# Two units of attention per round of TensorE: scores of both, projections, values of both

## The reference

```
# layer 1 (causal)                              # layer 3 (biased)
q, k, v = x @ W_Q, x @ W_K, x @ W_V             q, k, v = h @ Wq, h @ Wk, h @ Wv
s = where(causal, q k^T, -1e10) / sqrt(64)      s = q k^T / sqrt(16) + rel_bias[buckets]
x = layernorm(x + softmax(s) v W_O)             x = layernorm(x + softmax(s) v Wo)
```

## Time and profile before

| | us |
|---|---|
| median of 3 runs | 4693.07 (4691.93 to 4693.48) |
| the profiled execution | 4695.17 |
| its span, first to last instruction | 4693.4 |

### The profile page before, as it was taken

How to read it: one execution, slowest core, us unless ns; L and a number is a source line. 1 busy time by engine, 2 the same in 40 slices (tenths; PEclk the granted TensorE clock), 3 DMA queues, 4 the chain that set the end, 5 groups by cost and what they waited for, 6 DMA issues and landing times. The chain is left out here.

```text
span 4693.4 us, 63371 instructions
## 1 busy us (share of the span) xinstructions
PE 4113.2 (88%) x22554; PEld 2146.0 (46%) x22554; DVE 3458.5 (74%) x5816; ACT 1969.6 (42%) x3446; POOL 2788.1 (59%) x2036
## 2 busy tenths in 40 slices
PE   5999999999868999989999848999999999999964
PEld 3554454544445555555555424444444444444423
DVE  3877887878667777777877637887888788878836
ACT  2443443434445445445454313444344344434422
POOL 0655655556625677776786915665666566656640
PEclk6999999999978999999999958999999999999987
DMA  2000000000020000000000021211112111112111
GB/s 51 13 14 13 23 13 22 14 9 5 1 71 18 26 26 26 27 26 26 31 26 9 5 58 24 39 30 28 36 28 41 28 37 28 31 25 45 18 46 36
DMA packets 98041, 125.90 MB, mean 27 GB/s; under 512 B 28896, under 2 KB 76448, under 8 KB 97728
## 3 DMA queue, kind: packets, MB, share of 16 engines
q1 hardware_dynamic: 97728, 121.86, 11.8%
HBM read 103.69 MB, written 18.12 MB: 26 GB/s over the span
## 5 line engine op out<-in xcount | busy, mean ns | idle before, releaser
L729 POOL TENSOR_TENSOR s_psum_p<-s_psum_p,s_prob 128x1024 f32<-128x1024 f32 (+3 forms) x640 | 1350.2, 2110 | 415.5 <-ACT s_prob L476 376.7
L476 ACT ACTIVATE s_prob<-s_sT 128x1024 f32<-128x1024 f32 (+2 forms) x896 | 835.9, 933 | 970.4 <-DVE s_sT L610 479.8
L384 PE MATMUL s_pv<-s_prob,s_vp 128*64 128x512 f32 (+3 forms) x3584 | 889.0, 575 | 3.9 <-POOL s_prob L714 3.0
L729 POOL TENSOR_TENSOR s_psum_p<-s_prob 128x1024 f32<-128x1024 f32 (+1 forms) x128 | 286.9, 2241 | 573.5 <-ACT s_prob L476 570.8
L615 DVE RECIPROCAL s_recip<-s_recip 128x128 f32<-128x128 f32 x512 | 480.8, 941 | 99.3 <-ACT s_recip L426 99.3
L340 PE MATMUL s_mx<-s_bh,s_ah 64*128 64x512 f32 (+3 forms) x1792 | 390.7, 431 | 183.0 <-DVE s_bm L551 84.6
L1613 POOL TENSOR_TENSOR s_psum_p<-s_psum_p,s_prob 128x1024 f32<-128x1024 f32 x192 | 464.3, 2418 | 111.4 <-ACT s_prob L1340 109.5
L561 DVE CUSTOM_DVE_ANT_0 s_mx<-s_mx,s_strip 128x512 f32<-128x512 f32 x640 | 429.1, 711 | 111.9 <-PE s_mx L340 110.9
L1340 ACT ACTIVATE s_prob<-s_sT 128x1024 f32<-128x1024 f32 x256 | 262.6, 1026 | 478.0 <-PE s_sT L1200 474.1
L1455 DVE SCALAR_TENSOR_TENSOR s_part<-s_sT,s_gate,s_part 128x128 f32<-128x128 f32 x945 | 287.4, 322 | 213.1 <-ACT s_part L1332 180.6
L359 PE MATMUL s_sT<-s_ah,s_bh 64*128 64x512 f32 (+3 forms) x1792 | 414.4, 459 | 19.1 <-ACT s_prob L476 18.8
(11 more groups left out here) (251 smaller groups left out, 7560.4 us busy)
## 6 DMA issues: line engine op xcount, KB each, us to landing
s_strip<-bias_rows SPq DMA_DIRECT2D x256, 144.0 KB, 5.7
s_wr<-gated_weights SPq DMA_DIRECT2D x32, 960.0 KB, 4.8
s_near<-bias_rows SPq DMA_DIRECT2D x256, 48.0 KB, 2.0
x<-s_x SPq DMA_DIRECT2D x12, 512.0 KB, 3.2
s_x<-x SPq DMA_DIRECT2D x8, 512.0 KB, 4.7
gated_weights<-s_side_hi SPq DMA_DIRECT2D x8, 480.0 KB, 2.5
gated_weights<-s_side_lo SPq DMA_DIRECT2D x8, 480.0 KB, 2.9
s_x<-in_L_attn_x_dram SPq DMA_DIRECT2D x4, 512.0 KB, 4.3
```

The source lines that it names most:

```text
L384: last = mm(pv[heads(hd), lo:CH], vp[:, g % 2, j, heads(hd)], prob[:, k % PR, hd, lo:CH], start=j == 0, stop=end)
L476: nc.scalar.activation(prob[:, k % PR, :, lo:CH], sT[:, k % 2, :, lo:CH], ACT.Exp, scale=st.scale).then_inc(exp_done, 1)
L729: nc.gpsimd.tensor_tensor(out[:, :, lo:CH], src, p[:, :, lo:CH], ALU.add)\
```

## The change

The causal and the biased stage now walk their units two at a time ("a block"): units u and u+1 with u even. The gated stage keeps its own program.

- TensorE's order in a block: a chunk of maxima, scores of k, scores of k+1, a chunk of maxima, side jobs of the first unit, values of k-2 and of k-1, side jobs of the second unit.
- Every unit has exactly one chunk. A lead of 2 (causal) or 4 (biased) chunks of group g+2 is done in the last units of group g; the stage's prologue does them for group 1.
- "mt" becomes a side job and uses `misc` instead of `mx`; it stands at unit 10 (causal) or 12 (biased).
- The copy of the bias columns moves from VectorE to ScalarE (`bias_columns`, job "dc" at unit 8, semaphore `dc_done`), so `m_per` is 2.
- VectorE's order in a block: chunk of the first unit, near biases of both units, low part left from the block before, chunk of the second unit (and `head_maxima` after the last), side jobs of the first unit, then reciprocals, normalization and layer norm of both units.
- ScalarE's: both exponentials, side jobs of the first unit, copy of finished values, side jobs of the second unit, then "dc" and "cut".
- New places for the jobs. In an ordinary group: item 0, 4, 6, 8, v 2, 10, rs 3, 11 (biased); item 0, 2, 4, 6, v 5, 8, rs 3, 7 (causal). Reciprocals of a group's first pass at 13, 14, 14, 15 (biased) or 8 to 11 (causal), of its second pass in the next group at 5, 6, 6, 7. The first pass is normalized at unit 1 of the next group, the second at unit 7.

```diff
+        self.lead = 2 if causal else 4
+        self.mt_unit = 14
...
         if g + 1 < GP:
-            for u, count in enumerate(self.mx_steps):
-                out[u] += [("mx", g + 1, n + k) for k in range(count)]
-                n += count
-            out[self.mt_unit].append(("mt", g + 1))
+            for u in range(self.U - self.lead):
+                out[u].append(("mx", g + 1, u + self.lead))
+            out[self.U - self.lead].append(("mt", g + 1))
+            if self.biased:
+                out[8].append(("dc", g + 1))
+        if g + 2 < GP:
+            for n in range(self.lead):
+                out[self.U - self.lead + n].append(("mx", g + 2, n))
...
+        plan = {"item": (0, 4, 6, 8), "v": (2, 10), "rs": (3, 11)}
+        if turn:
+            plan = {"v": (1, 2), "xt": (3, 4), "rs": (5, 11), "item": (6, 7, 8, 9)}
+        elif after:
+            plan = {"item": (0, 2, 4, 6), "rs": (3, 11), "v": (5, 7), "y": (8, 10), "t": (14, 15)}
+        if self.causal:
+            plan = {"item": (0, 2, 4, 6), "rs": (3, 7), "v": (5, 8)}
+            if turn:
+                plan = {"v": (1, 2), "xt": (3, 4), "rs": (5, 7), "item": (6, 7, 8, 9)}
+            elif after:
+                plan = {"item": (0, 2, 4, 6), "rs": (3, 7), "v": (1, 5), "y": (8, 9), "t": (10, 11)}
...
-        for s, u in ((2 * g - 1, 3), (2 * g, rs1 + 1)):
-            if s >= 0:
-                for n in range(4):
-                    out[u + n].append(("recip", s, n))
-                out[u + 4 if u + 4 < self.U else u + 3].append(("norm", s))
+        if g > 0:
+            for n, u in enumerate((5, 6, 6, 7)):
+                out[max(u, plan["rs"][0] + 1)].append(("recip", 2 * g - 1, n))
+            out[7].append(("norm", 2 * g - 1))
+        for n, u in enumerate((8, 9, 10, 11) if self.causal else (13, 14, 14, 15)):
+            out[u].append(("recip", 2 * g, n))
+        if g > 0:
+            out[1].append(("norm", 2 * g - 2))
         if p == 1 and b > 0:
-            for n in range(7):
-                out[(3 if self.causal else 5) + n].append(("ln", b - 1, n))
+            for n, u in enumerate((3, 4, 5, 6, 7, 8, 10) if self.causal else (5, 6, 7, 8, 9, 10, 12)):
+                out[u].append(("ln", b - 1, n))
...
 # TensorE
-            for g, u, k, c, j, todo in units():
-                scores(g, u, k, c, j)
-                chunks = [t for t in todo if t[0] == "mx"]
-                for t in chunks[:1]:
+            for g, u, k, first, second in blocks():
+                for t in of_kind(first, ("mx",)):
                     maxima(t[1], t[2])
-                if k >= 2:
-                    values(k - 2)
-                for t in todo:
-                    if t[0] in MISC:
-                        misc_job(t)
-                for t in chunks[1:]:
+                for n in range(2):
+                    scores(k + n)
+                for t in of_kind(second, ("mx",)):
                     maxima(t[1], t[2])
-                if ("mt", g + 1) in todo:
-                    m_transpose(g + 1)
+                for t in of_kind(first, MISC):
+                    misc_job(t)
+                if k > 0:
+                    for n in range(2):
+                        values(k - 2 + n)
+                for t in of_kind(second, MISC):
+                    misc_job(t)
...
 # ScalarE
+            def bias_columns(g):
+                if g == 0:
+                    act.wait_ge(set_up, 2)
+                elif g >= 2:
+                    act.wait_ge(mt_full, g - 1)
+                hs = slice(2 * (g % NPAIR), 2 * (g % NPAIR) + 2)
+                copy(m8[:, g % 2, :, NB:3 * NB], dcol[:, hs, :, :].rearrange("p a b n -> p a (b n)"))\
+                    .then_inc(dc_done, 1)
...
+                for n in range(2):
+                    exponentials(k + n)
+                for t in of_kind(first, MISC):
+                    misc_job(t)
                 if tail_pass(k) is not None:
                     copy_values(tail_pass(k))
...
 # VectorE
-            for g, u, k, c, j, todo in units():
-                for t in todo:
+            for g, u, k, first, second in blocks():
+                for t in of_kind(first, ("mx",)):
+                    maxima(t[1], t[2])
+                for n in range(2):
+                    if st.near(*st.units[u + n]):
+                        near_biases(k + n)
+                for t in late:
+                    misc_job(t)
+                for t in of_kind(second, ("mx",)):
+                    maxima(t[1], t[2])
+                    if t[2] == NMX - 1:
+                        head_maxima(t[1])
+                for t in of_kind(first, MISC):
+                    misc_job(t)
+                for t in first + second:
                     if t[0] == "recip":
                         reciprocals(t[1], t[2])
...
-                late = [t for t in todo if t[0] in MISC]
+                late = of_kind(second, MISC)
+            normalize(2 * GP - 2)
```

More of the change, by code:

```diff
@@ L242, in units, with blocks, of_kind @@
                     yield g, u, g * U + u, c, j, schedule[g][u]
+        def blocks():
+            for g in range(GP):
+                for u in range(0, U, 2):
+                    yield g, u, g * U + u, schedule[g][u], schedule[g][u + 1]
+        def of_kind(todo, kinds):
+            return [t for t in todo if t[0] in kinds]
         def tail_pass(k):
             u = k % U
-            if u == 1 and k > 1:
+            if u == 0 and k > 0:
                 return 2 * (k // U) - 1
-            return 2 * (k // U) if u == st.at1 + 1 else None
+            return 2 * (k // U) if u == st.at1 else None
         block = ctx.enter_context(nc.Block())
@@ L288, in misc_job @@
                     last.then_inc(rs_full, 1)
+                    return
+                if job[0] == "mt":
+                    g = job[1]
+                    pe.wait_ge(m_step, m_per * (g + 1))
+                    if st.biased:
+                        pe.wait_ge(dc_done, g + 1)
+                    nc.tensor.transpose(misc[:, 0:P], m8[:, g % 2, :, :].rearrange("p a n -> p (a n)"),
+                                        cst.ident[:, :]).then_inc(mt_full, 1)
                     return
@@ L342, in maxima, with scores @@
                 last.then_inc(mx_full, 1)
[L344 to L349, removed]
+            def scores(k):
+                g, u = divmod(k, U)
+                c, j = st.units[u]
                 if k >= 2:
@@ L494, in _ @@
                 misc_job(("item", 1, k))
[L495 to L496 removed]
+            if st.biased:
+                bias_columns(0)
+            for g, u, k, first, second in blocks():
[3 more added lines that the diff above has]
+                    misc_job(t)
                 if tail_pass(k) is not None:
                     copy_values(tail_pass(k))
[L499 to L505 removed]
+                for t in of_kind(second, MISC):
+                    misc_job(t)
+                for t in of_kind(first + second, ("dc",)):
+                    bias_columns(t[1])
+                for t in of_kind(first + second, ("cut",)):
+                    act.wait_ge(raw_in, 16 * 6 * (t[1] + 1))
+                    act.wait_ge(cut_out, 32 * t[1])
+                    copy(side_hi[:, :], raw[:, :]).then_inc(cut_hi, 1)
             copy_values(2 * GP - 1)
@@ L518, in misc_job @@
                 if job[0] in ("rs", "v", "y"):
+                    return
+                if job[0] == "mt":
+                    max_rows(job[1])
                     return
@@ L667, in _ @@
             max_rows(0)
+            for n in range(st.lead):
+                maxima(1, n)
             late = []
-            for g, u, k, c, j, todo in units():
-                for t in todo:
+            for g, u, k, first, second in blocks():
+                for t in of_kind(first, ("mx",)):
[10 more added lines that the diff above has]
+                for t in of_kind(first, MISC):
+                    misc_job(t)
+                for t in first + second:
                     if t[0] == "recip":
                         reciprocals(t[1], t[2])
-                if st.near(c, j):
-                    near_biases(k)
-                for t in late:
-                    misc_job(t)
-                for t in todo:
-                    if t[0] == "mx":
-                        maxima(t[1], t[2])
-                        if t[2] == NMX - 1:
-                            head_maxima(t[1])
-                    elif t[0] == "mt":
-                        max_rows(t[1])
                     elif t[0] == "norm":
```

56 lines of the change are left out of this document (14 added, 42 removed).

## The result

The changed kernel takes 4776.55 us, median of 4 runs (4772.48 to 4785.39), against 4693.27 (4 runs) for the kernel before on the same chip. The ratio is 1.0179, 95% interval [1.0162, 1.0197]: 83 us slower, where I had forecast 24 us faster. The profiled execution has a span of 4775.2 us.

What follows compares the result with a forecast made beforehand. TensorE was taken to set the pace, with VectorE close. Ordinary groups -16 (biased) and -13 (causal), special groups +8 +11 +5 -9 and clock -10 gave -24 us: 4669 us, range 4590 to 4760.

Steps and rivals of the forecast that it cites:

- The switch, the blocks: TensorE, both stages: pairing units saves operand-shape switches, two units' values take 0.91 + 0.96 us; 0.35 us a block goes.
- Rival 4: Between two units' values the switch isn't saved, 1.01 us each: +34 us, about 4700, no change; chance 0.08.
- The walk of an ordinary group: Ordinary head-pair groups with their waits: biased 50.3 us against 50.86, causal 34.6 against 35.0; chance 0.55.
- Rival 3: VectorE's chain is shorter, TensorE's waits don't come: 4 us of waits instead of 6.7, 4560 us; chance 0.12.
- The normalization: VectorE, twice a group: 0.6 us at one end, 0.5 and a whole GpSimd addition (2.9) at the other.
- Rival 1: Each normalization falls just behind the start of a GpSimd addition: +144 us at full price, about 4770; chance 0.15.
- Special groups: Causal groups splitting weights +8 us, groups with layer norm +11, causal output projection +5, turned input -9.
- The new wait of the transpose back: Causal groups with the output projection: the transpose back waits for the rows of maxima, +5 us.
- TensorE's clock: Causal stage: half of some 20 us lost at 1.2 GHz is won back, -10 us, ends -20 and +50.
- rival 2: Biased stage: the clock falls at the new waits, to 0.98 or 0.97, about 4720 us; chance 0.10.

Runs made afterwards that it cites:

- the last one: Changed kernel with reciprocals spread over each group, VectorE's order chosen by kind of group, causal layer-norm instructions at other units: 4505.05 us, 0.9597 of the kernel before.

## Why the prediction was wrong

**The switch, the blocks.** Right: 1.87 us for two units' values. Rival 4 didn't happen.

**The walk of an ordinary group.** Right within 0.2 us biased (50.5 by the groups with one and two low stretches, 50.9 with the waits filled, against 50.3) and within 0.1 causal. Its waits came at the foreseen places. Rival 3 didn't happen. That it is so close is luck in part. The waits were shorter than foreseen and the rest longer: in the biased group above 6.1 us of waits against 6.7, so 44.4 against 43.7 for the rest, and in the causal group above 4.1 against 5.3, so 30.6 against 29.3. And the sentence that TensorE saves 2.8 us while its waits grow from about 3 to 6.7 doesn't give -0.5 us but +0.9; in the trace of before an ordinary biased group waited 2.9 us, so outside the waits TensorE saved 48.0 - 44.4 = 3.6 us.

**The normalization.** Rival 1 didn't happen. In the causal stage, where the rival set most of its price, the normalization took 0.82 us on average, against 1.49 before; in the biased one it took 1.42, and 1.39 before. VectorE by form, causal and then biased:

```profile
L654 DVE TENSOR_TENSOR s_z<-s_z,s_recip 128x512 f32<-128x512 f32 x60 | 49.4, 823 | 1.0
```
```profile
L654 DVE TENSOR_TENSOR s_z<-s_z,s_recip 128x512 f32<-128x512 f32 x63 | 89.7, 1424 | 1.1
```

The copy that moved to ScalarE had cost VectorE more than its size says: 2.10 us on average for 128x32 elements in the kernel before, 65 us in all. Part of that moved on to the instruction that now stands in its place, the small addition of `delta`, which took 0.15 us before and 0.73 after.

**Special groups.** The three causal groups with a layer norm cost +9.3, +5.8 and +8.1 us. They hold 13.6, 13.6 and 10.2 us at 1.2 GHz, where before only the second held 3.4. At half of the difference, the rate of the ordinary groups, the clock takes 7, 5 and 5 us of it, and what is left, 2.5, 0.7 and 3.0, is near the +2 that I gave. The new wait of the transpose back came: 6.6 us at three places in the whole kernel, where I had given it 5. The other terms for special groups were not measured apart from the clock.

**TensorE's clock: the step that failed.** I put it at -10 us, with ends of -20 and +50. At the same rate it was (157 - 3) / 2 = 77 us in the biased and (106 - 41) / 2 = 32 us in the causal stage, 109 in all, 119 from my value. By this estimate the change would stand at 82 - 109 = -27 us of the span without it; the other terms of my sum made -14. So the mechanism that I built the forecast on holds, and the term that I had put beside it, with the least work, decided the sign. This was rival 2, whose place and cause were right, but I gave it 0.10 and 4720 us where it came to 4776.

Two steps in the reasoning let that happen. I took the causal stage's clock of before, 0.98, as the price of "new waits"; but that number belongs to waits for the maxima of at most 1.4 us, one such wait in a group (8 of the stage's 11 stretches stand beside one), and the walk had just made waits of 1.1, 0.4, 1.7 and 1.7 within 20 us of each other. And I argued "the biased stage has wide matmuls on both sides of each", for which I had no row, because its clock of 1.00 belongs to a stage in which no wait for the maxima was over 0.9 us. The trace of before even had a row against it. TensorE waited for an exponential for 1.6 us three times in that stage, and beside the first of these waits, with matmuls 512 columns wide around it, lies its only stretch at 1.2 GHz (the values take 1.85 us there instead of 1.08):

```profile
3363.14 0.72 PE L359 MATMUL s_sT<-s_ah,s_bh 64*128 64x512 f32 x2 [1.60 <-ACT s_prob L476]
...
3365.07 1.85 PE L384 MATMUL s_pv<-s_prob,s_vp 128*64 128x512 f32 x4
```

An honest upper end was to be had from rows in hand: if the values behind each of two long waits a group run at half the clock, 0.91 + 0.96 us more each time, that is 32 x 2 x 1.87 = 120 us for the biased stage alone.

The 134 waits for the maxima in the changed kernel's biased stage hold 168 us, and the clock was 0.95; in the kernel before there were 143 that held 73 us, and it was 1.00. So it isn't how many there are; by the table above it is how long each is, and at 1.4 us also how close the last one was. The Trainium skill has this in "TensorE: Matmul & The Clock Gate", section "A second HAM failure mode: psum-queue depth-cycling": small idle times between groups of matmuls that come often enough make the clock go up and down between its levels. The traces agree in that it went up and down with no long idle time anywhere in the group, and differ in that as many shorter ones did nothing, while a single one of 2.1 us was enough. That section I should have weighed before the prediction.

## What to carry to other kernels

When a change turns short waits of TensorE into longer ones, price the clock before the waits: list each new wait with its length and its distance from the last one, look in the trace of before for waits of that length, whatever TensorE waited for, and what the clock did behind them, and take its fall behind each as the upper end. Spread what the waiting engine's partner does, rather than pack it: the same VectorE work, with two or three reciprocals in a block of most groups and the order of each kind of group chosen, took the kernel from 1.018 to 0.960 of the time before. And put the instruction that frees a shared buffer ahead of the ones that nobody waits for.

## What the runs showed of the hardware that I had not expected

- 118 us of useless matmuls, placed ahead of waits, made the kernel 46 us faster (4776.55 to 4730.61; by the ratios 0.0112, 53 us). The granted clock of the biased stage rose from 0.95 to 1.00.
- A single wait of TensorE of 2 us or more cost the clock nearly every time: 25 of 26 in the biased stage of the changed kernel, the six of 1.8 to 2.4 us in the last one.
- The groups fell into steps: 52.4 us with one stretch at 1.2 GHz, 54.2 to 54.3 with two.
- TensorE's busy time is no measure of its work: with the same matmuls it was 1461.7 us in the biased stage of the changed kernel and 1385.1 in the last one.
